# A decoder layer on one core: the first token tile's product with W_out moves from the attention stage to the end of the delta rule

## What is computed

```python
x = x + _L0_attn_ref(_layernorm(x, axis=-1), W_qkv, W_z, ..., W_out)    # gated delta rule, ends in o @ W_out
x = x + _L0_xattn_ref(_layernorm(x, axis=-1), ctx_512, ctx_512, Wc, bc)  # cross attention, 16 heads
x = x + _L0_ffn_ref(_layernorm(x, axis=-1), w_gate, w_up, w_down)        # block-quantised feed-forward
...
return o.reshape(Bb, Tt, VALUE_DIM) @ W_out          # end of _L0_attn_ref, VALUE_DIM = 2048
```

## Time and profile before

| what | value |
|---|---|
| median of 3 runs | 2134.35 us (2132.12 to 2138.12) |
| the profiled execution, its own time | 2132.07 us |
| its span | 2130.4 us |
| PE busy | 2001.5 us, 94% |
| DVE busy | 1710.0 us, 80% |
| ACT busy | 1500.8 us, 70% |
| mean granted clock of PE | 0.978 |

### The profile page before, as it was taken

The page is one execution under the profiler, slowest core; times in us unless marked ns, Lnnn a source line. Parts: engine busy times, 40 slices in busy tenths (PEclk is TensorE's granted clock), DMA queues, the critical chain, the costliest instruction groups (busy, mean ns, idle before and its releaser), DMA issues. The chain is left out here.

```text
span 2130.4 us, 54757 instructions
## 1 busy us (share of the span) xinstructions
PE 2001.5 (94%) x19285; PEld 1459.5 (69%) x19308; DVE 1710.0 (80%) x3957; ACT 1500.8 (70%) x4249; POOL 701.6 (33%) x601
## 2 busy tenths in 40 slices
PE   6799999999999999999999999969999999878998
PEld 3577777777777777777777777756666666554454
DVE  8687878878877877887887888854789998878997
ACT  2678878878888887887878888844666666654343
POOL 6411121121112112211211121121677777772332
PEclk8899999999999999999999999969999999999999
DMA  3000000000000100100000011114333333242111
GB/s 106 21 20 25 26 20 20 30 10 30 30 10 20 40 10 10 50 10 10 30 30 10 30 35 35 40 50 129 102 110 114 108 102 103 83 160 64 50 62 45
DMA packets 119589, 105.88 MB, mean 50 GB/s; under 512 B 12096, under 2 KB 94016, under 8 KB 119488
## 3 DMA queue, kind: packets, MB, share of 16 engines
q1 hardware_dynamic: 119488, 104.77, 15.9%
HBM read 70.66 MB, written 34.08 MB: 49 GB/s over the span
## 5 line engine op out<-in xcount | busy, mean ns | idle before, releaser
L771 PE MATMUL proj<-xn_hi,w_lo 128*128 x744 | 350.6, 471 | 0.0
L773 PE MATMUL proj<-xn_hi,w_hi 128*128 x744 | 293.8, 395 | 0.0
L772 PE MATMUL proj<-xn_lo,w_hi 128*128 x744 | 292.5, 393 | 0.0
L1177 DVE SCALAR_TENSOR_TENSOR qkv<-conv_in,taps,qkv 128x512 f32<-128x512 f32 x372 | 269.4, 745 | 0.0
L1424 POOL TENSOR_TENSOR o_scale<-o_var,neg_half 128x4 f32<-128x4 f32 x66 | 66.5, 1024 | 526.6 <-DVE o_var L1207 526.5
L1440 POOL TENSOR_TENSOR k_len<-sumsq,pos_half 128x4 f32<-128x4 f32 x31 | 45.4, 1464 | 556.3 <-DVE sumsq L1365 556.3
L1305 DVE TENSOR_TENSOR i_less_r<-bank_c,join_mask 128x256 f16<-128x256 f32 x320 | 120.7, 418 | 94.5 <-PE bank_c L834 93.8
L1087 ACT ACTIVATE inv<-bank_b 128x256 f16<-128x256 f32 x320 | 108.1, 382 | 87.6 <-PE bank_b L855 84.1
L773 PEld LDWEIGHTS proj<-xn_hi,w_hi 128*128 128x128 f32 x744 | 139.9, 188 | 32.6
L1998 ACT ACTIVATE probs_t<-ps_s 128x512 f32<-128x512 f32 x128 | 69.6, 596 | 130.4 <-PE ps_s L1813 130.4
L1032 ACT ACTIVATE g_mask<-mask_ge,g_cols 128x128 fp32r<-128x128 f32 x512 | 153.3, 408 | 8.3 <-DVE g_cols L1397 8.3
(11 more groups left out here) (326 smaller groups left out, 5766.2 us busy)
## 6 DMA issues: line engine op xcount, KB each, us to landing
out_t<-o_out SPq DMA_DIRECT2D x66, 256.0 KB, 2.0
w_hi<-out_t SPq DMA_DIRECT2D x32, 512.0 KB, 5.5
w_raw<-in_L_attn_W_qkv_dram SPq DMA_DIRECT2D x32, 256.0 KB, 2.8
wq_dram<-wq_q SPq DMA_DIRECT2D x48, 128.0 KB, 2.0
x_sb<-in_x_dram SPq DMA_DIRECT2D x16, 256.0 KB, 2.7
w_raw<-in_L_attn_W_z_dram SPq DMA_DIRECT2D x16, 256.0 KB, 2.7
w_raw<-in_L_attn_W_out_dram SPq DMA_DIRECT2D x16, 256.0 KB, 2.7
x_in<-in_x_dram SPq DMA_DIRECT2D x16, 256.0 KB, 5.8
```

The costliest lines, as they stand in the source:

```text
L771: pe.matmul(out, w_lo[:, k, cols], sh.xn_hi[:, k, tok], start=(k == 0), stop=False)
L772: pe.matmul(out, w_hi[:, k, cols], sh.xn_lo[:, k, tok], start=False, stop=False)
L773: product = pe.matmul(out, w_hi[:, k, cols], sh.xn_hi[:, k, tok], start=False, stop=(k == KT - 1))
L1177: dve.scalar_tensor_tensor(out=out, in0=conv_in[:, j, :, k:k + T], scalar=taps[:, j, k:k + 1], in1=out, op0=ALU.mult, op1=ALU.add).then_in ...
```

## The change

One PSUM tensor, `carried.bank`, is made before all stages. In `delta_rule` it is `bank_c[0]`, in `attend` it is `ps_y`, in `feed_forward` it is `ps_d`. The 48 matmuls of tile (0, 0) leave `attend` and become `first_tile` in `delta_rule`: the first 18 (six parts) are put after the last step and before the two `to_channels`, the other 30 (ten parts) behind them. In `attend`, PE raises `o_used` and `y_ps[0]` at once instead. SP issues x of tile (0, 0) ahead of the raw outputs of tile (0, 1).

```diff
     def __init__(self, nc, ctx):
+        self.bank = ctx.enter_context(nc.psum_tensor("bank", [P, 4, P], F32))
...
-        bank_c = [st.enter_context(nc.psum_tensor(f"bank_c{s}", [P, 4, P], F32)) for s in S]
+        bank_c = [carried.bank, st.enter_context(nc.psum_tensor("bank_c1", [P, 4, P], F32))]
...
                 step(STEPS, None, None)
+
+                def first_tile(first, last):
+
+                    for part in range(first, last):
+                        e, g = part // KE, part % KE
+                        if part == 0:
+                            pe.wait_ge(o1_done[0], STEPS + 1 + FIRST)
+                            pe.wait_ge(w_lo_done, TILES * HK + WO)
+                        if g == 0:
+                            pe.wait_ge(o_lo_done, e + 1)
+                        k, y = 2 * g + e, bank_c[0][:, :, :].rearrange("p h t -> p (h t)")
+                        pe.matmul(y, o_lo[e][:, g, :], out_weight(sh.xn_hi, k), start=(part == 0), stop=False)
+                        pe.matmul(y, o_hi[e][:, g, :], out_weight(sh.xn_lo, k), start=False, stop=False)
+                        pe.matmul(y, o_hi[e][:, g, :], out_weight(sh.xn_hi, k), start=False, stop=(part == WO - 1))
+
+                first_tile(0, KE - 2)
                 for s in S:
                     to_channels(STEPS + 1, s, False)
+                first_tile(KE - 2, WO)
...
-        ps_y = st.enter_context(nc.psum_tensor("ps_y", [P, D], F32))
+        ps_y = carried.bank[:, :, :].rearrange("p h t -> p (h t)")
...
+                load_x(0, 0)
                 load_outputs(0, 1, 0)
-                load_x(0, 0)
...
-                project(0, 0, PIECES // 2)
+
+                pe.sem_inc(o_used, 1)
+                pe.sem_inc(y_ps[0], 1)
                 pe.wait_ge(wc_in, 48)
...
-        ps_d = st.enter_context(nc.psum_tensor("ps_d", [P, D], F32))
+        ps_d = carried.bank[:, :, :].rearrange("p h t -> p (h t)")
```

More of the change, by code:

```diff
@@ L571, in delta_rule @@
         FIRST = 1
-        WO = HV
+        WO, KE = HV, HV // 2
         o_raw, o_hi, o_lo = carried.outputs()
```

## The result

The changed kernel takes 2138.22 us in the median of 14 runs, the kernel before 2134.28 us. The ratio is 1.0016, 95% interval [1.0009, 1.0023]: 3.4 us slower (1.9 to 4.9), less than the 0.3% that was set as the bound of "the same", but clear of zero. The forecast was +2.9 us.

What follows compares the result with a forecast made beforehand. The attention's steps were taken as bound by PE, so the end follows PE's arrival. Terms +1.2 (loop start), -0.4 (sum of tile (0, 0)) and +2.1 (clock) gave +2.9 us: 2134.35 to 2137.2 us, range 2131 to 2143.

Steps and rivals of the forecast that it cites:

- The mark and what it moves: First key transposes in the attention, at 1462.01: forecast to move by +2.9 us, and the kernel's end by as much.
- rival 5: Attention steps: loads shifted against PE by a few us could give or take some us either way; chance 0.09.
- 18 matmuls at no cost: Delta rule, ahead of the transposes: 18 matmuls take 4.1 us at the full clock and fit under POOL's wait.
- rival 4: Delta rule: the 18 matmuls overrun POOL's wait, transposes up to 2 us late; chance 0.12 together with rival 1.
- 30 matmuls, 6.8 us at the high clock: Delta rule, behind the transposes: 30 matmuls at 0.227 us each end at about 1436.9, after the store's landing.
- Rival 1: Delta rule's end: the clock falls, the 30 matmuls start cold, +2.1 us; chance 0.12 together with rival 4.
- The stage's late start: Start of the attention: PE now ends the delta rule, so the stage begins at 1438.5, 3.6 us later.
- The bare wait: Attention's head: PE waits uncovered for Wc and bias row until 10.6 us into the stage; transposes start +1.2 us.
- The clock behind the wait: Wc loop: after 12 us idle PE runs at half speed for 4.3 us, +2.1 us.
- The sum of tile (0, 0), -0.4: Wc loop: DVE's sum for tile (0, 0) comes sooner, so PE's 0.43 us wait goes, -0.4 us.
- Rival 2: Wc loop: the clock does not come back, the whole loop runs at half speed, +12.7 us; chance 0.06.
- rival 3: Attention's head: Wc is there when PE asks, so the mark comes 9 us sooner (2125); chance 0.03.

Runs made afterwards that it cites:

- e3: Changed kernel plus 44 extra matmuls (results not used) ahead of PE's wait for Wc; ratio 1.0001 to the kernel before.
- e5: Kernel before plus 30 extra matmuls (results not used) behind the transposes of the delta rule; ratio 1.0028, +6.0 us.
- e1: Changed kernel with only the first 18 matmuls in the delta rule, the other 30 back at the attention's head; ratio 0.9986, 3.0 us faster than before.
- e2: Changed kernel with the bias row on its own semaphore, so PE waits only for the two DMAs of Wc; ratio 1.0013 to before.
- e7: Changed kernel with 33 matmuls in the delta rule, Wc halves on separate semaphores, bias row last, 18 extra matmuls, DVE's sum before its split; ratio 0.9989 to before.
- e10: Changed kernel with 33 matmuls in the delta rule (18 ahead of the transposes, 15 behind), 15 at the attention's head; ratio 1.0009 to before.

## Why the prediction was right

- **The mark and what it moves.** E is 329.7 us in every kernel, so the steps take up nothing of the head's growth, and rival 5, a shift in their phase, falls for E. That the growth reaches the end is shown by the medians (seven of ten follow the head to 0.8 us), and not by the profiled pair: there S takes 2.5 of the 3.0 us back and F and G add 3.9, S by the clock of that execution, F and G at least in part by it. Whether the change has a share in F and G stays open.
- **18 matmuls at no cost: nearly.** I took the high clock from the trace of before and got 4.1 us; both traces of the changed kernel had the low one at first, and in the first of them the 18 took 6.1 us. The term was mis-sized by 2.0 us. The transposes for s = 0 began 0.4 us late (1429.67, POOL's first product at about 1429.25), but those for s = 1 wait for POOL's second product anyway, so the cost at the stage's start was nothing: A is 16.2 us with the low clock here and with the high one in e3, and rival 4 cost nothing here. What was wrong is that I took the clock of one trace for the clock of every execution. The clock at that place differs between executions of one kernel: in the first profile of before it was 1.00 from 1422.5 to 1424, in the second 0.50.
- **30 matmuls, 6.8 us at the high clock:** 6.9 measured. Rival 1 (they start cold) did not come to pass. e5 shows that they do start cold without the 18 ahead of them, which costs 1.5 us (8.65 against 7.1). e3's trace has the very pause that the rival was about, 1.34 us and then transposes, and the clock held.
- **The stage's late start:** 3.6 us predicted, 16.2 - 12.8 = 3.4 measured (3.3 in the second pair). The seam took 1439.27 - 1437.84 = 1.4 us from PE's last matmul, where I took 1.7.
- **The bare wait:** 10.6 us predicted, 10.3 measured; e1, which covers it, is faster than before. But the bias row is only the last 0.5 us of it (e2), and not the 1.5 us that I expected of e2; without it PE waits for Wc.
- **The clock behind the wait:** 2.1 us predicted, 2.6 in e3 against the changed kernel. The low clock lasted 5.2 us, longer than the 4.3 of the earlier trace rows.
- **The sum of tile (0, 0), -0.4:** the warm loop is 13.4 us in e3 and 14.1 before, so -0.7.
- **The sum:** 3.4 + (10.3 - 13.05) + (16.0 - 14.1) = +2.5 us at the first key transposes against +2.9. D is 0.5 us longer, because the transposes of the queries run at the low clock, but this is mostly a shift: the low stretch there lasts about 6.8 us in both traces (PEclk 0.65 and 0.67 in the windows from 1465 and from 1470 before; 0.85, 0.50 and 0.96 in those from 1465, 1470 and 1475 after), and only begins sooner behind the key transposes. Rival 2 (the clock does not come back in the loop) and rival 3 (Wc is there at once) are both ruled out by this trace. In rival 2 the 48 matmuls at 0.20 us more come to 9.6 to 9.7 us, not 9.8, which changes nothing.
- **How much of the hit is luck.** The terms add up to +2.5 at the mark and the ratio gives 3.4 (1.9 to 4.9), so the mechanism carries the forecast. That the median lies within 0.5 us of it is more than the method can promise: one execution differs from another of the same kernel by 4 us, and e5, e7 and e10, forecast in the same way, missed by about 2 to 5 us.

## What to carry to other kernels

Work moved across a barrier into idle time pays only as far as two things still cover each other: what ends the earlier stage, and what the work used to hide in the later one. Here 48 matmuls hid a DMA wait of 10 us; moved as a whole they delayed the stage by 3.4 us and bared the wait, moved by half and with the DMAs in the order of need they gained 4.3 us. And if TensorE would stand idle before a stretch that it bounds (here 4.3 us were enough, 1.6 were not, and 2.4 us went either way), price that stretch at the low clock, or leave it something to do.

## What the runs showed of the hardware

- Two kernels whose stage start and landing of the DMAs agree within 0.4 us, e1 and e10, differ by 2.3 us in the next loop. What differs ahead of it is how long PE had been idle (1.6 and 6.6 us). In e10 the granted clock fell in a window where PE did nothing, and it stayed low for the beginning of the next stretch.
- Extra matmuls in idle time (e3) made a loop 2.6 us shorter by the clock alone. The Trainium skill, TensorE: Matmul & The Clock Gate, section "HAM oscillation — how this bites in real kernels", describes the loss behind a DMA wait; this case's traces agree, with 16.0 against 13.4 us for the same loop.
- The same wait of 2.40 us for the same instruction was followed by the low clock in one trace (0.50 from 1494 to 1496 in the kernel before) and by the high one in another (1.00 from 1498 to 1500 in the changed kernel).
- The clock can fall without a long pause. In the changed kernel it was 0.94 from 1419 to 1421 and 0.50 from 1421 to 1422.5, and between 1417 and 1421 PE did 2.24 us of work in groups with waits of 0.83 and 0.86 us between them.
- The clock's course differs between executions of one kernel where PE has pauses. At the head of the feed-forward of the kernel before it was 1.00 from 1930 to 1960 in one execution, and 0.83 and then 0.91 in the other; the stage took 202.7 and 204.8 us. A pair of profiles can so differ by 4 us for no reason of the kernel (spans of 2130.4 and 2134.4), more than the change itself.
